# Row scatters of three routing stages: a wait on the landing four places back in place of one hold per step

## The reference

```
x = x + attention(layernorm(x))          # 16 heads, terraced and linear part
x = x + moe(layernorm(x))                # 16 experts, top 2, and one shared expert
x = x + memories(layernorm(x))           # gated linear attention on 4 routed memories, top 2, and a shared one
x = x + moe(layernorm(x))                # the same experts again
```

## Time and profile before

| | us |
|---|---|
| median of three runs | 2658.96 |
| the profiled execution | 2684.99 |
| its span, first to last instruction | 2683.3 |
| PE busy in the span | 2124.7 (79%) |
| DVE, ACT, POOL busy | 1836.9, 1561.9, 1531.6 |
| first expert stage, first to last scatter | 1311.0 to 1413.8 |
| memory stage, first to last scatter | 1599.7 to 1704.9 |
| second expert stage, first to last scatter | 2397.6 to 2497.3 |

### The profile page before, as it was taken

How to read it: one execution, slowest core, us unless ns; L and a number is a source line. 1 busy time by engine, 2 the same in 40 slices (tenths; PEclk the granted TensorE clock), 3 DMA queues, 4 the chain that set the end, 5 groups by cost and what they waited for, 6 DMA issues and landing times. The chain is left out here.

```text
span 2683.3 us, 111106 instructions
## 1 busy us (share of the span) xinstructions
PE 2124.7 (79%) x45872; PEld 1600.7 (60%) x45872; DVE 1836.9 (68%) x4507; ACT 1561.9 (58%) x3824; POOL 1531.6 (57%) x3168
## 2 busy tenths in 40 slices
PE   8788888888888888888868944389999998687793
PEld 5456566566566665556637734366766776565682
DVE  6578888887878887884544555276777777575456
ACT  5577777777777777772433322266666665454231
POOL 3357666666766666768554546544444444256452
PEclk9889999999999999999988965699999999789897
DMA  6911111111121111113346654301111111542546
GB/s 216 265 33 40 40 40 40 40 40 40 41 63 39 40 40 40 40 29 120 138 113 209 197 172 153 109 22 47 51 50 51 49 41 35 199 169 89 154 146 225
DMA packets 188851, 245.89 MB, mean 92 GB/s; under 512 B 41672, under 2 KB 144981, under 8 KB 187456
## 3 DMA queue, kind: packets, MB, share of 16 engines
q1 hardware_dynamic: 161824, 182.08, 22.7%
q0 software_dynamic: 19872, 50.41, 5.5%
q10 hardware_dynamic: 6656, 6.31, 0.8%
HBM read 136.08 MB, written 106.50 MB: 90 GB/s over the span
## 5 line engine op out<-in xcount | busy, mean ns | idle before, releaser
L666 ACT ACTIVATE at_E<-at_S,at_mn 128x1024 f32<-128x1024 f32 (+7 forms) x704 | 594.2, 847 | 211.3 <-DVE at_mn L737 178.2
L737 DVE TENSOR_REDUCE at_mn<-at_S 128x1 f32<-128x1024 f32 (+3 forms) x448 | 494.0, 1104 | 152.6 <-PE at_S L846 152.3
L846 PE MATMUL at_S<-am_sk,am_sq 96*32 96x512 bf16 (+3 forms) x4608 | 395.8, 350 | 1.1 <-ACT at_Tt L656 1.0
L887 PE MATMUL at_pcs<-at_E,at_c 128*32 128x256 f32 (+1 forms) x4864 | 375.7, 338 | 0.0
L605 POOL TENSOR_TENSOR at_kvo<-am_kh,am_vh 128x256 f32<-128x256 f32 x512 | 304.2, 628 | 0.0
L887 PEld LDWEIGHTS at_pcs<-at_E,at_c 128*32 128x32 f32 x4864 | 229.7, 109 | 41.2 <-issue 0.2
L1360 POOL DMA_INDIRECT expert_out<-m_ysb,m_dst x158 | 155.5, 984 | 139.3 <-issue 76.7
L887 PE MATMUL at_pcs<-at_Tt,at_c 128*32 128x128 f32 x1024 | 189.8, 274 | 42.3 <-ACT at_pcs_s L679 42.3
L590 POOL TENSOR_TENSOR at_half<-at_half 128x128 f32<-128x128 f32 (+4 forms) x640 | 185.6, 290 | 50.1
L864 PE MATMUL at_M<-am_ident,at_Tt 128*32 128x64 f32 x8192 | 154.5, 225 | 68.9 <-ACT at_kvr L691 43.1
L656 ACT ACTIVATE at_Tt<-at_S,at_mn 128x192 f32<-128x192 f32 x512 | 174.1, 428 | 48.3 <-DVE at_mn L725 48.1
(11 more groups left out here) (393 smaller groups left out, 5579.9 us busy)
## 6 DMA issues: line engine op xcount, KB each, us to landing
m_xg<-expert_rows SPq DMA_DIRECT2D x158, 129.0 KB
am_sq<-q_parts SPq DMA_DIRECT2D x192, 64.0 KB, 2.3
am_sk<-k_parts SPq DMA_DIRECT2D x192, 64.0 KB, 2.3
memory_rows<-m_blank SPq DMA_DIRECT2D x16, 516.0 KB
gl_hx<-memory_rows SPq DMA_DIRECT2D x32, 258.0 KB, 3.6
m_wgu<-in_f_wgu SPq DMA_DIRECT2D x2, 4096.0 KB
rt_yin<-expert_out SPq DMA_DIRECT2D x7, 1024.0 KB, 11.4
fn_yin<-expert_out SPq DMA_DIRECT2D x7, 1024.0 KB, 8.9
```

The lines of the kernel that those rows point to most:

```text
L666: ins = nc.scalar.activation(E[:, at:at + w], S[v % NS_B][:, i * CW:i * CW + w], ACT.Exp, bias=mn[:, q, s, 1 + j:2 + j], scale=-1.0, accum ...
L737: nc.vector.tensor_reduce(mn[:, q, :, :].rearrange("p s k -> p (s k)")[:, at[0]:at[0] + 1], S[v % NS_B][:, 0:w], AX.X, ALU.min).then_inc(s ...
L846: ins = nc.tensor.matmul(S[v % NS_B][x, at:at + cw], sq[:, u, t * P + x.start:t * P + x.stop], sk[:, u, c0 + c:c0 + c + cw], start=True, s ...
L887: ins = nc.tensor.matmul(pcs[j * R:(j + 1) * R, cols[0]:cols[1]].rearrange("p (b c) -> p b c", c=P), lhsT, rhs, start=(n, j) not in touche ...
```

## The change

One semaphore per place in a ring of four (`FLIGHT`) takes the place of the single `sent`. Scatter i of a stage (0 to 63) counts on semaphore i modulo 4, and from scatter 4 on POOL waits ahead of it until scatter i - 4 has landed. The hold at the head of a step is gone. SP waits at the end for four semaphores, sixteen scatters each. Nothing else changes: order, targets and number of the scatters are as before.

```diff
@@ -1175,6 +1175,9 @@
 NTILE = (T * TOPK + NE * (P - 1)) // P
 
 
+FLIGHT = 4
+
+
 def phase_moe(nc, acc, tw, gate, w_gu, w_down, xs, yb, memory_rows, x_out, tag, hx, K):
 
     with ExitStack() as ctx:
@@ -1243,7 +1246,7 @@
         s_T, s_hT, s_log, s_ex, s_chain = (m.sem(k) for k in ("T", "hT", "log", "ex", "chain"))
         s_top, s_e2, s_sel, s_run, s_cnt, s_slot = (m.sem(k) for k in ("top", "e2", "sel", "run", "cnt", "slot"))
         s_gu, s_act, s_hid, s_dn, s_acc, s_mine = (m.sem(k) for k in ("gu", "silu", "hid", "dn", "acc", "mine"))
-        sent = m.sem("sent")
+        sent = [m.sem(f"sent{u}") for u in range(FLIGHT)]
         s_n, s_tab, s_spread, s_pad = m.sem("n"), m.sem("tab"), m.sem("spread"), m.sem("pad")
         pad_out = [m.sem("pad_out0"), m.sem("pad_out1")]
         got = [m.sem(f"got{u}") for u in range(NB)]
@@ -1277,7 +1280,8 @@
                 at = sp.value_load(pad_at[0:1, e:e + 1], min_val=0, max_val=HOME - P)
                 sp.dma_start(xs[ds(at, P), :], empty[:, :]).then_inc(pad_out[0], 16)
             sp.wait_ge(s_tab, 11)
-            sp.wait_ge(sent, 2 * NTT * 16)
+            for u in range(FLIGHT):
+                sp.wait_ge(sent[u], TOPK * NTT // FLIGHT * 16)
             sp.wait_ge(dummy_out, 16)
             for u in range(2):
                 sp.wait_ge(pad_out[u], NE // 2 * 16)
@@ -1348,12 +1352,13 @@
                     pool.wait_ge(s_hn, (n + 1 - K) * G)
                 pool.wait_ge(s_e2, n + 1)
                 pool.wait_ge(s_slot, n + 1)
-                if n:
-                    pool.wait_ge(sent, n * G * TOPK * 16)
                 for t in range(n * G, (n + 1) * G):
                     for j in range(TOPK):
+                        i = t * TOPK + j
+                        if i >= FLIGHT:
+                            pool.wait_ge(sent[i % FLIGHT], i // FLIGHT * 16)
                         pool.indirect_dma_start(out=xs, out_offset=bass.IndirectOffsetOnAxis(ap=slot[:, t, j:j + 1], axis=0),
-                                                in_=hx[:, t, :], in_offset=None).then_inc(sent, 16)
+                                                in_=hx[:, t, :], in_offset=None).then_inc(sent[i % FLIGHT], 16)
             for t in range(NTILE):
                 pool.wait_ge(s_dst, t + 1)
                 pool.wait_ge(s_y, t + 1)
@@ -1796,7 +1801,8 @@
                 sp.wait_ge(hT_out[u], NS // 2 * 16)
             sp.wait_ge(kept_out, 16)
             sp.wait_ge(weights_in, len(weights) * 16)
-            sp.wait_ge(sent, NTT * TOPK * 16)
+            for u in range(FLIGHT):
+                sp.wait_ge(sent[u], TOPK * NTT // FLIGHT * 16)
 
         @block.gpsimd
         def _(pool):
@@ -1839,13 +1845,14 @@
                 pool.wait_ge(s_hn, (n + 1) * G)
                 pool.wait_ge(s_e2, n + 1)
                 pool.wait_ge(s_slot, n + 1)
-                if n:
-                    pool.wait_ge(sent, n * G * TOPK * 16)
-                for t in range(first_tile(n), first_tile(n) + G):
+                for k, t in enumerate(range(first_tile(n), first_tile(n) + G)):
                     for j in range(TOPK):
+                        i = (n * G + k) * TOPK + j
+                        if i >= FLIGHT:
+                            pool.wait_ge(sent[i % FLIGHT], i // FLIGHT * 16)
                         pool.indirect_dma_start(out=gx, out_offset=bass.IndirectOffsetOnAxis(ap=slot[:, t, j:j + 1], axis=0),
                                                 in_=hx[:, t, :], in_offset=None, bounds_check=B * NM * CAP - 1,
-                                                oob_is_err=False).then_inc(sent, 16)
+                                                oob_is_err=False).then_inc(sent[i % FLIGHT], 16)
 
         @block.scalar
         def _(act):
```

## The result

The changed kernel took 2630.06 us (median of 4 runs, 2626.37 to 2631.45), the kernel before 2659.02 beside it (2658.64 to 2667.83): a ratio of 0.9887, 95% interval 0.9871 to 0.9903, 29.0 us less. The forecast was 2640.1 us, 18.9 less, with a range from 2633 to 2648.

What follows compares the result with a forecast made beforehand. Holds between POOL's scatter steps were taken to bound the three stages, then pads, slots or POOL's issue rate. Gains of 7.7 + 9.0 + 2.2 = 18.9 us took 2658.96 to 2640.1 us, range 2633 to 2648.

Steps and rivals of the forecast that it cites:

- Removed holds, added waits: All three stages: seven holds a stage go, about 2.0 us each in quiet stretches; added satisfied waits cost zero.
- rival (a): Added waits: each satisfied one costs the 0.73 us restart, 33 us lost in all, 2692 us; chance 0.06.
- (d): Scatters lengthen where they overlap other work, 1.2 us against 0.96; the gain is gone, 2659 us; chance 0.04.
- (b): Four in flight throttle wherever other transfers run: gains 5 first stage, 6 memory, 0 last; 2648 us; chance 0.15.
- Step 0: Opening of the first expert stage, beside the weight load: scatter 4 waits for a landing, the step ends 3.9 us later.
- First expert stage: First expert stage's scatters: pads are late next, at about 1407 us; gain 7.7 us, bounds 6 and 12.
- Memory stage: Memory stage's scatters: step 7 starts at 1686.0 where it started at 1695.0; gain 9.0 us, bounds 7 and 9.
- Second expert stage: Second expert stage: scatters move by 7.8 us, but pads limit; gain 2.2 us, bounds 0.5 and 4.
- Rival (c): Expert stages: pads don't limit, ending earlier; gains 11 first, 6 last, with 9.0 for memory; 2633 us; chance 0.12.
- The carry: Whole kernel: the median stays 26.0 us below the profiled execution, so 2658.96 - 18.9 = 2640.1 us.

Runs made afterwards that it cites:

- experiment 5: Kernel before with landings counted on four semaphores, each step still held until all have landed: 0.9999 of the kernel before (0.9985 to 1.0013).
- first series: The first comparison, unmodified changed kernel beside the kernel before on one chip: 2630.06 us against 2659.02, ratio 0.9887.
- experiment 6: The changed kernel once more, unmodified, in a later series beside the kernel before at 2677.75 us: 1.0081 (1.0063 to 1.0100), 22 us slower.
- The other kind of series: Four middle series, kernel before at medians of 2675.6 to 2688.3 us; the whole change, run in one of them, took 1.0081 of it.
- experiments 1 to 16: Kernel before again, the change in single stages or whole, and variants of hold, flight, pace and scatter contents; kernel before at medians of 2675.6 to 2688.3 us.

## Why the prediction was wrong, point by point

- **Removed holds, added waits**: right. Behind the start of step 1, or of step 3 in the memory stage, and until the pads set in, every gap of the changed kernel is 0.30 us. A satisfied wait costs nothing that these rows show; rival (a) is out, and experiment 5 says the same for the counting. The means of the scatters didn't grow, so (d) is out too. Of (b) only the stretching beside the pads came, 5.6 us in the first expert stage and 2.6 in the second; from step 3 on in the memory stage there was none.
- **Step 0**: right in kind. Scatter 4 starts 3.6 us behind scatter 3 in place of 1.26, and the three waits of step 0 add 2.4 + 2.0 + 0.6 = 5.0 us where I had 3.9. Counted from the first scatter, step 1 began 3.8 us later in the first expert stage and 3.2 in the second, step 2 only 1.0 us later and at the same time: the holds that are gone cover it, in the second stage wholly, as forecast.
- **First expert stage**: 7.7 forecast, 7.9 measured, but for another reason. The pads didn't limit; they went out 66.0 us after the first scatter in place of 76.5, and stretched the scatters of step 6 (gaps of 1.69 and 2.80 us) in place of outlasting those of step 7. That the number fits is in part luck.
- **Memory stage**: 9.0 forecast, 9.1 measured; 49.9 us behind the scale computation where the text said 51.
- **Second expert stage**: 2.2 forecast, 8.8 measured. This is the step that failed, with 6.6 of the 10 us: "So only the last 0.5 to 1.5 us was the scatters' alone". The scatters moved by the 7.8 us of the forecast (first to last start 98.7 us before, 90.9 after); the pads were to take most of that back, and took nothing. In the profile of before the pads left 84.2 us after the first scatter (2481.86 - 2397.6), since the slots of that execution followed each other at 11.7 us; after the change they left at 66.7 us (2425.73 - 2359.07). I took the lateness of the slots for a property of the stage, and so the pads for the next thing late. It is none: with the scatters back to back the slots came at 9.3 us in the first series and at 12.6 in experiment 6. Whether they come in time in the kernel before where it takes 2659 us isn't known. Rival (c) had the place right, "`xg` directly behind the scatters", and its 2633 is 3 us off; its terms were 11 and 6 for the expert stages, where 7.9 and 8.8 came.
- **The carry**: I moved the 26.0 us between the profiled execution and the median over as a constant, without asking where they lie. By the traces that was right: the rest of the span, outside the stages, differs by 28.7 us between the two profiles, and the stages add up to 312.7 us in the profile and to some 315, the estimate above, at the median. I had no row for it, so that it held is luck.
- **The 3.2 us that are left** of the gain can't be placed for certain, since no execution of the kernel before at 2659 us was profiled. By the estimate above they are in the stages (315 against 286.9 after, 28 us).
- **The other kind of series** was in none of the rivals. There the same change costs 22 us, it seems by a mechanism that the profile of before had in it at a small scale. The exponentials of a step stood 3 us late on ACT, released as POOL came to its hold (the timeline of ACT, kernel before):

```profile
1332.69 1.28 ACT L1393 ACT_TABLE_LOAD   x1
1337.03 0.22 ACT L1393 ACTIVATE m_ex<-m_b 128x64 f32<-128x64 f32 x1 [3.06 <-DMA mg_qT<-q_full]
```

Five of them came 1.9 to 3.3 us late in this way in the two expert stages, and each started between the end of a step's last scatter and the start of the next step's first, while POOL issued nothing. I had read the intervals of the slots and not asked why they were uneven.

## What to carry to other kernels

When the profiled execution is 1% off the median, first ask where that 1% lies; here it was outside the stages in question. A stage whose intervals are longer than its work is still not a base for saying what is late next. An engine that issues back to back is not only a cost of its own; when a pause is taken out, look at what the other engines get done in it, and try the new pace in more than one series before trusting a gain. Where a hold and a pace do the same, the pace (here 0.22 us of POOL a scatter) shows which of the two is needed.

## What the runs showed of the hardware

- In four of six series (experiments 1 to 16) TensorE's results reached DVE and ACT late, by 8 to 9 us in the rows shown, while POOL issued scatter instructions every 1.20 to 1.39 us. They came in time at 1.48 us and with arithmetic in the place of the scatters; fewer bytes (32 in place of 1032 a row) and fewer rows (64 or next to none in place of 128) didn't cure it. In the first series 1.26 us did no harm, in the last 1.41 us.
- In these four series the trace has no median landing time for the scatters, as if part of their landing records were missing. The Trainium skill, NOTIFIC — the notification-queue block, section 7.1 (Overflow: three behaviours, one of which stalls the engine), says that the path which carries such records can push back on the engine that makes them, and also that neither of the two overflow marks was ever seen set in its measurements. By that rule the recording itself would hold TensorE back, since every scatter adds the same 16 landing signals whatever it moves. That would fit the experiments of these series. No run here shows it: no execution without records was made, and what makes a series one of the two kinds stays open.
